# Output products of a gated cross-attention kernel: two of three 256-column products become one of 512 columns, and the steps are ordered anew

## The reference, cut to what matters

```python
# cross attention, added to x
q_hk   = (layernorm(x) @ Wq.T).reshape(b, s, H, K)
q_big  = einsum('bshk,hkq->bshq', q_hk, w_kc_q)
kv     = rope(ctx)
q_r    = einsum('bshq,hqr->bhsr', q_big, W_qr)
k_r    = einsum('bld,hdr->bhlr', kv, W_kr)
attn   = softmax(einsum('bhsr,bhlr->bhsl', q_r, k_r))
ctx_c  = einsum('bhsl,bld->bhsd', attn, kv)
ctx_l  = einsum('bhsd,hkd->bshk', ctx_c, w_kc_kv)
x      = x + tanh(g_xattn) * (ctx_l.reshape(b, s, H * K) @ Wo.T)
# the network: y = layernorm(x), thought from its last row, four steps
thought = layer_norm(y)[:, -1] @ agg_w + agg_b
4 times: thought += gelu(layer_norm(thought) @ d1_w + d1_b) @ d2_w + d2_b
broadcast = thought @ bc_w + bc_b
out    = layer_norm(y + sigmoid(y @ gate_w + gate_b) * broadcast)
x      = x + tanh(g_ffn) * out
```

## Time and profile before

| | |
|---|---|
| time, median of 3 runs | 220.52 us (219.85 to 221.07) |
| the profiled execution's own time | 219.46 us |
| its span, first to last instruction | 217.7 us |
| TensorE busy | 202.2 us, 2533 products |
| VectorE busy | 171.2 us, 407 instructions |
| ScalarE, GpSimd busy | 104.3 us, 76.4 us |
| mean granted TensorE clock | 0.986 |
| moved by DMA | 17.87 MB, mean 82 GB/s |

### The profile page before, as it was taken

One profiled execution on the slowest core, in us unless ns is written; L12 is line 12 of the kernel. 1 busy time (PEld: TensorE's weight loads), 2 busy tenths in 40 slices (PEclk: granted clock), 3 DMA queues, 4 the chain that ended last, 5 costly groups with the idle time before them and its releaser, 6 DMA issues.

```text
span 217.7 us, 6284 instructions
## 1 busy us (share of the span) xinstructions
PE 202.2 (93%) x2533; PEld 174.3 (80%) x2533; DVE 171.2 (79%) x407; ACT 104.3 (48%) x191; POOL 76.4 (35%) x161
## 2 busy tenths in 40 slices
PE   7699999899999999989999999999999999998960
PEld 5388889678879988877889897898988999886930
DVE  4146489999985888999688599696758789989884
ACT  2255775566465248307535665609534543625120
POOL 8932002012999639899010110010003205244251
PEclk9979999999999999999999999999999999999997
DMA  5999994529218414000400040000400300011001
GB/s 150 238 250 244 345 202 183 107 94 261 35 30 215 138 61 99 0 3 0 102 3 0 5 99 3 0 0 6 101 3 6 97 20 9 10 41 29 24 24 48
DMA packets 21716, 17.87 MB, mean 82 GB/s; under 512 B 5524, under 2 KB 19892, under 8 KB 21688
## 3 DMA queue, kind: packets, MB, share of 16 engines
q1 hardware_dynamic: 21688, 17.47, 32.4%
HBM read 12.16 MB, written 1.05 MB: 61 GB/s over the span
## 4 chain that ended last, share of the span: by engine, by line
PE 48%; DVE 31%; POOL 8%; issue 6%; DMA 3%; ACT 2%; SPq 0%; POOLq 0%; DVEq 0%; ACTq 0%
DVE row_max L1032 5%; PE ps L1299 5%; PE ps L1331 5%; PE ps L1167 4%; PE ps L1318 4%; PE ps L1169 4%; PE ps L1168 4%; PE ps L1320 4%; DMA x<-in_x 3%; DVE bn L948 3%; DVE q_split L1024 2%; PE ps L1423 2%; DVE q_split L1026 2%; PE ps L1216 2%; DVE ctxn L1045 2%
## 5 line engine op out<-in xcount | busy, mean ns | idle before, releaser
L911 ACT ACTIVATE probs<-ps 128x512 f32<-128x512 f32 x64 | 36.6, 596 | 27.1 <-PE ps L1320 26.5
L817 POOL TENSOR_SCALAR var_eps<-mean_var 128x1 f32<-128x1 f32 (+1 forms) x29 | 6.9, 238 | 113.0 <-DVE mean_var L949 112.8
L1032 DVE TENSOR_REDUCE row_max<-ps 128x2 f32<-128x512 f32 x64 | 42.3, 682 | 0.6 <-PE ps L1299 0.4
L1331 PE MATMUL ps<-kv,probs 128*64 128x65 f32 x1024 | 33.9, 223 | 0.0
L1331 PEld LDWEIGHTS ps<-kv,probs 128*64 128x64 f32 x1024 | 31.4, 137 | 2.9 <-issue 2.2
L1318 PE MATMUL ps<-q_hi,kv_lo 128*128 128x512 f32 x64 | 27.7, 433 | 0.0
L1299 PE MATMUL ps<-kv_hi,q_split 128*128 128x256 f32 x128 | 26.0, 299 | 0.9 <-DVE q_split L1026 0.8
L1320 PE MATMUL ps<-q_split,kv_hi 128*128 128x512 f32 x64 | 25.2, 394 | 0.0
L1299 PEld LDWEIGHTS ps<-kv_hi,q_split 128*128 128x128 f32 x128 | 19.8, 189 | 4.7 <-DVE row_max L1032 1.6
L1167 PE MATMUL ps<-B_lo,ctxT_hi 128*128 128x256 f32 x64 | 18.7, 292 | 0.7 <-DVE ctxT_lo L1049 0.7
L1167 PE MATMUL ps<-xT_lo,A_hi 128*128 128x256 f32 x64 | 18.8, 293 | 0.4 <-DVE q_split L1026 0.3
(11 more groups left out here) (149 smaller groups left out, 441.8 us busy)
## 6 DMA issues: line engine op xcount, KB each, us to landing
q_hi<-q_split SPq DMA_DIRECT2D x16, 256.0 KB, 4.2
wq<-in_L_xattn_Wq SPq DMA_DIRECT2D x4, 512.0 KB, 9.9
wo<-in_L_xattn_Wo SPq DMA_DIRECT2D x2, 1024.0 KB, 10.2
w_rest<-in_L_ffn_d_w SPq DMA_DIRECT2D x2, 1024.0 KB, 5.5
wkcq<-in_L_xattn_w_kc_q SPq DMA_DIRECT2D x8, 192.0 KB, 5.3
out_x<-fin SPq DMA_DIRECT2D x8, 128.0 KB
wqr<-in_L_xattn_W_qr SPq DMA_DIRECT2D x4, 192.0 KB, 5.4
x<-in_x SPq DMA_DIRECT2D x8, 64.0 KB, 5.7
```

The source lines that it names most:

```text
L911: act.activation(probs[:, n % PROBS_BUFS, lb, :], bank(e), ACT.Exp).then_inc(free[place[e]], 1)
L1032: dve.reduce_max(row_max[:, s % 2, 2 * j:2 * j + 2], bank(e).rearrange("p (h l) -> p h l", h=2), AX.X).then_inc(free[place[e]], 1)
L1331: ins = pe.matmul(bank(e)[q:q + 64, hh * (DC + 1):(hh + 1) * (DC + 1)], probs[:, n % PROBS_BUFS, lb, hh * P + q:hh * P + q + 64], kv1[:, k ...
```

## The change

B's two parts lie in one tile, lo first. For each i, context hi is multiplied with both parts at once: one product of 512 columns whose moving operand is the 256 columns of B_lo and the 256 of B_hi (8 KB apart), into the two halves of a bank. Context lo times B_hi, 256 columns, is added to the first half as before. So a unit has 16 products in place of 24, and its bank holds two halves to be summed: VectorE does a second scaled add, which waits for the first. The bank is freed by the second.

```diff
-        B_hi = sb("B_hi", [P, H // 2, D], F32R)
-        B_lo = sb("B_lo", [P, H // 2, D], F32R)
+        B = sb("B", [P, 2, H // 2, D], F32R)
+        B_lo, B_hi = B[:, 0], B[:, 1]
...
                     xu = x[:, x_tile(u), :]
-                    ins = dve.scalar_tensor_tensor(xu, bank(out_e)[:, 0:D], g_tanh[:, 0:1], xu, ALU.mult, ALU.add)
+                    link(dve.scalar_tensor_tensor(xu, bank(out_e)[:, 0:D], g_tanh[:, 0:1], xu, ALU.mult, ALU.add))
+                    ins = dve.scalar_tensor_tensor(xu, bank(out_e)[:, D:2 * D], g_tanh[:, 0:1], xu, ALU.mult, ALU.add)
                     ins.then_inc(free[place[out_e]], 1)
...
+            def wide_product(e, i):
+
+                pe.matmul(bank(e), ctxT_hi[:, i, :], B[:, :, i, :], start=(i == 0), stop=False)
+                return pe.matmul(bank(e)[:, 0:D], ctxT_lo[:, i, :], B_hi[:, i, :], start=False,
+                                 stop=(i == H // 2 - 1))
...
                     for i in range(H // 4):
-                        split_product(bank(e)[:, 0:D], ctxT_hi[:, i, :], ctxT_lo[:, i, :], B_hi[:, i, :],
-                                      B_lo[:, i, :], i == 0, False)
+                        wide_product(e, i)
...
                     for i in range(H // 4, H // 2):
-                        ins = split_product(bank(out_e)[:, 0:D], ctxT_hi[:, i, :], ctxT_lo[:, i, :], B_hi[:, i, :],
-                                            B_lo[:, i, :], False, i == H // 2 - 1)
+                        ins = wide_product(out_e, i)
```

The rest of the diff is the table `SLOTS`, written anew for all five engines. Two lines of it, of SyncE's part:

```diff
-        "load_x_rest": (76,),
+        "load_x_rest": (91,),
...
-        "load_ffn": (129,),
+        "load_ffn": (227,),
```

More of the change, by code:

```diff
@@ L51 @@
     "pe": {
[L52 to L87, removed]
@@ L102 @@
[L102 to L112, removed]
@@ L113 @@
-        "f_pre": (310, 347, 375, 390, 395, 410, 416, 419),
-        "keep": (414,),
-        "f_norm": (358, 372, 378, 402, 405, 417, 421, 422),
+        "load_ident": (16,),
+        "load_wkcq": (3, 8, 12, 13, 21, 28, 97, 114),
+        "load_wqr": (11, 24, 58, 110),
+        "load_wkr": (9,),
+        "load_wq": (10, 22, 25, 29),
+        "load_x": (42, 105),
+        "load_x_rest": (165,),
+        "load_rope": (2,),
+        "load_ctx": (15,),
+        "load_wo": (44, 51),
+        "load_wkckv": (253,),
@@ L116 @@
+        "f_y": (130, 285, 328, 355, 372, 379, 411, 413),
+        "f_pre": (233, 330, 376, 385, 401, 410, 418, 419),
+        "keep": (416,),
+        "f_norm": (323, 360, 389, 400, 409, 415, 421, 422),
     },
     "dve": {
[L118 to L124, removed]
-        "load_rope": (8,),
@@ L143 @@
[L143 to L152, removed]
@@ L178 @@
[L178 to L181, removed]
+        "load_ident": (30,),
+        "load_wkcq": (1, 5, 16, 18, 29, 31, 53, 60),
+        "load_wqr": (9, 15, 94, 98),
+        "load_wkr": (11,),
+        "load_wq": (54, 61, 63, 114),
+        "load_x": (14, 39),
+        "load_x_rest": (262,),
+        "load_rope": (8,),
+        "load_ctx": (25,),
@@ L182 @@
+        "f_y": (238, 331, 356, 373, 380, 387, 401, 417),
+        "f_pre": (329, 361, 365, 374, 393, 408, 416, 419),
+        "keep": (421,),
+        "f_norm": (344, 371, 378, 384, 400, 414, 420, 422),
     },
     "act": {
[L184 to L191, removed]
@@ L244 @@
-        "f_y": (322, 337, 365, 379, 391, 398, 401, 419),
-        "f_pre": (349, 368, 370, 393, 400, 406, 414, 420),
-        "keep": (416,),
-        "f_norm": (356, 381, 383, 395, 407, 412, 421, 422),
+        "load_ident": (20,),
+        "load_wkcq": (6, 9, 25, 26, 27, 52, 70, 91),
+        "load_wqr": (14, 61, 110, 141),
+        "load_wkr": (51,),
+        "load_wq": (12, 81, 82, 136),
+        "load_x": (19, 28),
+        "load_x_rest": (336,),
+        "load_rope": (5,),
+        "load_ctx": (4,),
@@ L248 @@
+        "f_y": (307, 355, 358, 370, 388, 391, 410, 420),
+        "f_pre": (314, 361, 381, 395, 404, 408, 416, 421),
+        "keep": (419,),
+        "f_norm": (345, 373, 394, 399, 409, 413, 418, 422),
     },
     "pool": {
-        "load_ident": (4,),
-        "load_wkcq": (5, 7, 11, 14, 17, 27, 29, 41),
-        "load_wqr": (8, 42, 43, 55),
-        "load_wkr": (21,),
-        "load_wq": (20, 46, 64, 92),
-        "load_x": (16, 37),
-        "load_x_rest": (79,),
-        "load_rope": (3,),
@@ L310 @@
-        "f_y": (281, 316, 356, 363, 387, 405, 408, 418),
-        "f_pre": (299, 362, 371, 389, 398, 407, 415, 421),
-        "keep": (417,),
-        "f_norm": (369, 381, 392, 393, 401, 414, 419, 422),
+        "load_ident": (68,),
+        "load_wkcq": (7, 8, 25, 27, 34, 37, 46, 54),
+        "load_wqr": (18, 19, 87, 103),
+        "load_wkr": (5,),
+        "load_wq": (1, 47, 134, 171),
+        "load_x": (12, 91),
+        "load_x_rest": (39,),
+        "load_rope": (38,),
+        "load_ctx": (0,),
@@ L380 @@
+        "f_y": (219, 222, 302, 354, 371, 391, 409, 412),
+        "f_pre": (230, 325, 376, 387, 390, 405, 416, 418),
+        "keep": (421,),
+        "f_norm": (342, 378, 384, 395, 408, 413, 417, 422),
     },
```

426 lines of the change are left out of this document (234 added, 192 removed), and 60 rows, old and new, of the table SLOTS.

## The result

The changed kernel takes 221.12 us (median of 12 executions, 219.3 to 222.4), the kernel before beside it 219.77 (12 executions, 217.6 to 222.2): ratio 1.007, 95% interval 1.004 to 1.010. Forecast was 0.8 us less than before, too little to be told from no difference; it is about 1.5 us more. 221.1 lies within the range of 217.9 to 222.0, but on the side of the rival that said slower.

A forecast was written before the change was run, and what follows sets the result against it. TensorE mostly sets the pace, VectorE in 90:100 and 178:200. Product -0.1, second add +2.0, orders -3.3 and new waits +0.6 sum to -0.8 us: 219.7 us from the median of 220.52, range 217.9 to 222.0.

The forecast's parts named there:

- The product: TensorE's output units: one 512-column and one 256-column product take about as long as three of 256; -0.1 us.
- rival 4: TensorE's output units: a wide product streams faster than two narrow ones, up to 7.6 us less, 212.9 us; chance 0.02.
- The second add: VectorE, 0.51 us per unit: units 0, 2, 3, 4 covered by idle time, units 1, 5, 6, 7 paid; +2.0 us.
- The orders: Reordered steps on all engines remove waits at the front, unit 1, gq 3.2, after unit 5 and the tail; -3.3 us.
- new waits: +0.3 us for agg_w landing late at agg 0, and +0.3 us estimated for other new neighbours in the lists.
- front: Before smax 0.1: x_stats 2 and x_norm 2 move ahead, shortening TensorE's 0.77 us wait; -0.5 us (0 to -1.1).
- unit 1: Near 101.26 us: VectorE work moves after smax 4.0, so TensorE's smax 4.1 waits less; -0.95 us (0 to -0.95).
- gq 3.2: At 131.47 us: row maximum smax 5.1 moves behind the subtraction that frees TensorE's bank; -0.45 us (0 to -0.65).
- After unit 5 and the tail: smax 7.7 and f_y 1 move before unit 5's add, -0.9; unit 7's later statistics hidden behind GpSimd's f_y 6, -0.5.
- agg_w: Load issued later on SyncE, landing near 86.8 to 89 us where agg 0 wants it at 87.20; +0.3 us (0 to +2).
- Rival 2: VectorE's second add is the bound in 90:100 and 178:200, only front and tail given back: +1.5, 222.0 us; chance 0.18.
- Rival 1: Orders give all they can and the new waits don't come: -1.9 to -2.6, some 218.3 us; chance 0.33.

The follow-up runs named there:

- e5: Kernel before, old orders, with the wide product but without its second add (second bank half left out): ratio 1.003, -0.15 us at equal low time.
- e7: Kernel before, three products kept, scaled add done twice at units 0, 2, 3 and 4 only: ratio 1.007, +1.35 us at equal low time.
- e1: Changed kernel's wide product and second add, with the orders of the kernel before: ratio 1.016 to the kernel before, +2.6 us at equal low time.
- e6: Kernel before, three products kept, scaled add done twice at all eight units: ratio 1.014, +2.9 us at equal low time.
- e2: Kernel before with only the new orders, old product and single add: ratio 1.003, -1.0 us at equal low time.
- e15: Second run of the kernel before with only the new orders, old product and single add: ratio 1.000, -0.9 us at equal low time.
- e9: Kernel before, extra add at units 0, 2, 3 and 4 reading x, bank freed by the first add: ratio 1.001, +1.3 us at equal low time.
- e12: Kernel before with the new orders only up to smax 0.1 on every engine: ratio 1.003, +0.2 us at equal low time.
- e3: The changed kernel measured again, unaltered, with a second profile: ratio 1.006 to the kernel before, +1.0 us at equal low time.
- e8: Kernel before, three products kept, scaled add done twice at units 1, 5, 6 and 7 only: ratio 1.006, +1.25 us at equal low time.
- e4: Changed kernel with the store of f_norm 0 put back behind q_hi_load 7: ratio 1.005 to the kernel before, +0.7 us at equal low time.
- e14: Changed kernel with the three bc_rows steps set apart, each behind a pv step: ratio 1.004 to the kernel before, +1.6 us at equal low time.

## Why the prediction was right or wrong

- **The product, -0.1: right.** e5 has -0.15 us. A wide product starts 0.23 us before its follower, and rival 4 is out. By the estimate from the spacings in the Trainium skill (TensorE: Matmul & The Clock Gate, section Back-to-back issue gap) the change would have brought 4.2 us; the trace (0.23 us) and e5 don't bear it out.
- **The second add, +2.0: this step failed.** "The adds of units 0, 2, 3 and 4 follow steps that TensorE does in 74:83 and 120:170, where VectorE's 1.1 and 12.5 idle us cover them: nothing." In the old orders they cost 1.35 us (e7), and all eight 2.8 to 2.9 (e1 against e5; e6). VectorE's idle time in a stretch says that its work fits, not that nobody waits for the next result: its list is in order, and TensorE was already waiting on it right behind the adds of some units. The four that I did price came to 1.25, under 2.0. In the new orders all eight cost 1.9, as much as forecast, but not at the places forecast: unit 3's, which I had at nothing, costs 0.5 at gq 3.3. No run splits the units there, so that the total agrees may be luck.
- **The orders, -3.3, and new waits, +0.6: their size failed too.** Net -2.7 was forecast. With the adds in, +2.6 (e1) became +1.1: -1.5; alone they brought -1.0 and -0.9 (e2, e15), and by the plain ratios nothing. The starts in the table say where. Up to gate 1 the changed kernel gains 1.6 us on e1, where front and unit 1 were priced at 1.45: the front has its 0.6 at gq 1.1 (0.5 priced), of which 0.3 is left at 87; between there and pv 2.2 unit 1 brings 0.8 (0.95 priced, of which the 0.45 at smax 4.1 was a wait that e1, e5, e7, e9 and e12 don't have even in the old orders), and 0.6 more comes up to gate 1, which waits 0.29 us for the add in e1 and not in the changed kernel. The *gq 3.2* gain is 1.48 - 0.99 = 0.5 at yT 2, as priced, and is gone again at pv 4.0: the steps behind it wait for other results. From gate 1 to pv 5.2 the orders gain 0.3 on e1. And the front has a new wait that I put at nothing: VectorE for the load of x, up to 2.01 us, and TensorE 1.05 behind it in e3. How often it comes no run says.
- **After unit 5 and the tail, -1.4: not these sizes.** From pv 5.2 to the end I had +1.5 for three adds and -1.4 for the orders, +0.1; the profiles have 48.95 us before and 49.12 in the changed kernel, +0.17. The sum agrees by luck: in the old orders three adds cost 0.7 there (e8, 49.63), so the orders gave back 0.5. In the changed kernel st 7.0.0 is 0.09 us later than before although TensorE had stood ready for it for 0.88 us. I had looked for a new wait at just this step, from the issue of q_hi_load 7 behind a store, priced 0 to +0.6; the order did no harm (e4), but the small DMA of maxima landed in 2.9 us instead of 1.9. The last stretch, from unit 5's first add at 179.05, is 38.45 us, within the 38 to 39 forecast.
- **The tail.** Unit 7's statistics end at 207.00 and GpSimd, done with f_y 6 at 206.70, takes them up at 207.09, after 0.39 idle; before it was 206.76. So "that extra is hidden" holds for most of it, not all.

The timeline of VectorE and GpSimd that this rests on:

```profile
205.96 0.74 POOL L842 TENSOR_TENSOR x<-x,out_beta 128x256 f32<-128x256 f32 x1
206.82 0.18 DVE L949 BATCH_NORM_AGGREGATE mean_var<-bn 128x2 f32<-128x6 f32 x1
207.09 0.22 POOL L817 TENSOR_SCALAR var_eps<-mean_var 128x1 f32<-128x1 f32 x1 [0.39 <-DVE mean_var L949]
```

- **agg_w: its +0.3 wasn't needed**; agg 0 waits for VectorE only.
- **The rivals.** Rival 2 came, with its sign and nearly its size (+1.5 forecast, +1.1 at equal low time), but not by its place alone: in the old orders half of the adds' price fell in the stretches that it leaves out, and two of the gains that it denies, unit 1 and gq 3.2, are seen in the profile. Rivals 1, 3, 4 and 5 did not. (Rival 1's end, and with it the range's, should read -2.4: -0.8 - 0.6 - 2 x 0.5.)

The account with the forecast's own terms, forecast and in brackets found at equal low time: product -0.1 (-0.15), adds +2.0 (+2.8), orders and waits -2.7 (-1.5); sum -0.8 (+1.1). The adds' miss is 0.8, the orders' 1.2. Counted the other way round, orders first (e2, e15), then the adds in the new orders, it is orders -0.95, adds +1.9: then the whole miss is the orders'. The 0.9 us between the two ways is what orders and adds share; that the orders were priced far too high holds in both.

What stays open: where the changed kernel's typical execution loses its 1.1 us, since behind agg 0 both of its profiles take as long as the one before (the wait for x seen in e3 is a candidate, and would also fit e12, whose time shows no gain); and whether the wait at st 7.0.0 can be had back by moving the fetch. Neither was tried.

## What to carry to other kernels

Idle time of an engine in a stretch doesn't cover an instruction put into its list: look right behind the place for the first result that another engine waits for, and if anyone waits on that line already, charge the instruction in full. Price it in the new order, not only in the old: here the same adds cost 2.8 us in one and 1.9 in the other. Where an addition moves from the accumulating matrix engine to a vector engine and the columns stay the same, nothing is gained and the addition is paid. And a gain from a reordering counts only as far as the next wait: list that one too, down to the small DMAs, and the loads that an instruction moved forward may now have to wait for. A gain read from one execution may be a wait that the next doesn't have.

## What the hardware showed that I had not expected

- An instruction fetch and a kernel's own small copy may get in each other's way: with a packet of 0.02 MB of the instruction queue in the same microsecond an 8 KB copy lands in 2.4 to 3.2 us (seven profiles), without in 1.8 to 1.9 (eleven). That one causes the other was not tried. The Trainium skill (Runtime: NRT & Kernel Launch, section Instruction fetch mechanics) has an engine's instructions come in blocks of 16 KiB through a queue of its own, at a cost mostly hidden. The size agrees; whether a fetch costs the engine itself anything no run here shows, but the copy beside it landed 1 us later.
- TensorE, busy without a gap from 166 to 174 us, can be granted 1.2 GHz behind ten products of 4 rows in one block (e15 and seven other profiles of fourteen), and has 2.4 GHz throughout in the four where pv stands between them. A fall there costs about 1.4 us: in e1 the distance from the kernel before goes from +1.51 at pv 5.2 to +2.93 at st 6.0.1. Low time behind 205 us, in the tail, costs nothing that can be seen (32.7 us from st 7.0.0 to the end with 5.5 us of it in the changed kernel and with 3.0 in e14).
